# Moving half of VectorE's look-ahead statistics behind the normalising step in a fused group-norm and hexagonal convolution

## The reference

```python
g = v.reshape(B_, 32, C_ // 32, H_, W_)
gn = (g - mean(g)) / sqrt(var(g) + 1e-5)          # over each group of 2 x 256 values
xp = pad(gn, 1);  xp[:, :, DST_R, DST_C] = xp[:, :, SRC_R, SRC_C]     # 30 wrapped edge points
up    = conv(xp, w_up * _UP, b_up)                 # 5 taps each, stride 2, 64 -> 64 channels
left  = conv(xp, w_left * _LEFT, b_left)
right = conv(xp, w_right * _RIGHT, b_right)
out[:, :, 0::2, 0::2], out[:, :, 1::2, 0::2], out[:, :, 1::2, 1::2] = up, left, right
return x + out * OUT_MASK
```

## Time and profile before

| | |
|---|---|
| median of the runs | 735.11 us |
| profiled execution | 734.9 us |
| its span | 733.1 us |
| PE busy | 655.4 us (89%) |
| DVE busy | 617.0 us (84%) |
| ACT busy | 575.0 us (78%) |
| POOL busy | 473.3 us (65%) |
| moved between HBM and SBUF | 269.65 MB, mean 368 GB/s |
| granted TensorE clock, mean | 0.992 of full speed |

### The profile page before, as it was taken

How to read it: one execution, slowest core, us unless ns; L and a number is a source line. 1 busy time by engine, 2 the same in 40 slices (tenths; PEclk the granted TensorE clock), 3 DMA queues, 4 the chain that set the end, 5 groups by cost and what they waited for, 6 DMA issues and landing times.

```text
span 733.1 us, 36312 instructions
## 1 busy us (share of the span) xinstructions
PE 655.4 (89%) x15484; PEld 602.6 (82%) x15484; DVE 617.0 (84%) x1793; ACT 575.0 (78%) x1235; POOL 473.3 (65%) x1109
## 2 busy tenths in 40 slices
PE   1699999999999989889898898898988988988993
PEld 1589999999999888788788887887888878878883
DVE  4999999999999888798888888878988988878740
ACT  3498888988888787877877877878778778787782
POOL 1177777787777756757657557566576575675774
PEclk9999999999999999999999999999999999999997
DMA  8999999999999999999999999999999999999998
GB/s 265 348 360 384 384 384 379 373 375 372 370 370 373 371 375 372 365 373 374 371 381 381 368 376 377 371 361 376 378 375 377 375 375 376 372 362 374 383 353 285
DMA packets 271100, 269.65 MB, mean 368 GB/s; under 512 B 8720, under 2 KB 270864, under 8 KB 271056
## 3 DMA queue, kind: packets, MB, share of 16 engines
q1 hardware_dynamic: 270576, 269.25, 106.6%
q10 hardware_dynamic: 480, 0.00, 0.0%
HBM read 135.01 MB, written 134.22 MB: 367 GB/s over the span
## 4 chain that ended last, share of the span: by engine, by line
DVE 36%; DMA 25%; POOL 18%; ACT 12%; issue 3%; PE 3%; SPq 2%; POOLq 0%
DMA xs<-in_x 25%; DVE stats L246 19%; POOL xs L418 13%; ACT tn L330 12%; DVE tn L294 8%; POOL tn L428 5%; PE bank L476 3%; DVE small L278 2%; SPq L197 2%; DVE small L282 2%; DVE rstd L285 2%; DVE nmr L289 1%; DVE mate L254 1%; DVE var L267 0%; DVE small L275 0%
## 5 line engine op out<-in xcount | busy, mean ns | idle before, releaser
L476 PE MATMUL bank<-tn,wts 64*64 64x192 f32 (+1 forms) x15360 | 646.6, 325 | 0.0
L476 PEld LDWEIGHTS bank<-tn,wts 64*64 64x64 f32 x15360 | 593.2, 136 | 34.0
L246 DVE BATCH_NORM_STATS2 stats<-xs 128x6 f32<-128x512 f32 x512 | 350.6, 697 | 84.8 <-DMA xs<-in_x 84.4
L418 POOL TENSOR_TENSOR xs<-res,xs 128x192 f32<-128x192 f32 (+6 forms) x775 | 375.1, 528 | 5.7 <-ACT res L353 4.6
L330 ACT ACTIVATE tn<-xs,nmr,rstd 128x256 f32<-128x256 f32 x511 | 258.9, 592 | 74.1 <-DVE nmr L289 73.6
L353 ACT ACTIVATE res<-bank,bias 64x512 f32<-64x512 f32 (+5 forms) x640 | 302.1, 472 | 18.1 <-PE bank L476 7.7
L428 POOL COPY tn<-tn 128x128 f32<-128x128 f32 (+2 forms) x320 | 97.9, 362 | 238.2 <-ACT tn L330 238.2
L294 DVE TENSOR_SCALAR tn<-xs,rstd,nmr 128x256 f32<-128x256 f32 x513 | 180.3, 424 | 2.3
L487 PEld LDWEIGHTS bank<-blank 128*128 128x128 f16 x64 | 6.1, 96 | 76.3 <-ACT res L353 58.7
L487 PE MATMUL bank<-blank 128*128 128x2 f16 x64 | 11.2, 176 | 57.8 <-POOL tn L428 57.8
L324 ACT ACTIVATE std<-var 128x16 f32<-128x16 f32 x64 | 13.8, 216 | 50.7 <-DVE var L267 50.7
(11 more groups left out here) (18 smaller groups left out, 24.0 us busy)
## 6 DMA issues: line engine op xcount, KB each, us to landing
xs<-in_x SPq DMA_DIRECT2D x256, 512.0 KB, 8.0
out<-xs SPq DMA_DIRECT2D x256, 512.0 KB, 8.3
tn<-in_L_conv_w_up SPq DMA_DIRECT2D x1, 256.0 KB, 3.6
tn<-in_L_conv_w_left SPq DMA_DIRECT2D x1, 256.0 KB, 4.1
tn<-in_L_conv_w_right SPq DMA_DIRECT2D x1, 256.0 KB, 5.5
bias<-in_L_conv_b_up ACTq DMA_DIRECT2D x2, 0.2 KB, 4.5
bias<-in_L_conv_b_left ACTq DMA_DIRECT2D x2, 0.2 KB, 5.6
bias<-in_L_conv_b_right ACTq DMA_DIRECT2D x2, 0.2 KB, 7.3
```

What stands on the lines that cost most here:

```text
L246: last = nc.vector.bn_stats(stats[:, k % 2, 2 * u:2 * u + 2].rearrange("p g a -> p (g a)"), both)
L418: last = nc.gpsimd.tensor_tensor(onto, frm, onto, ALU.add)
L476: last = nc.tensor.matmul(psum[bank + j][to:to + C, at:at + cols], wts[first:first + C, NT * rect[0] + n, :], taps(b, rect, tap, first), s ...
```

## The change

In `moments` and `norms` DVE now takes only the first four of the next chunk's eight `bn_stats`, one in each of four places. The other four, with their wait for the second half of that chunk's load, follow `normalise(k)`.

```diff
-                bn(ahead, 2, 4)
+                bn(ahead, 2, 3)
 
             def norms(k, ahead):
                 dve.wait_ge(std_ready, k + 1)
                 nc.vector.reciprocal(small[:, 0], std[:]).then_inc(stat_step, 1)
-                bn(ahead, 4, 5)
+                bn(ahead, 3, 4)
                 dve.wait_ge(stat_step, done + 1)
                 nc.vector.scalar_tensor_tensor(small[:, 1], ...)
-                bn(ahead, 5, 6)
                 dve.wait_ge(stat_step, done + 2)
                 nc.vector.tensor_tensor(small[:, 2], ...)
-                bn(ahead, 6, 7)
                 dve.wait_ge(stat_step, done + 3)
                 nc.vector.scalar_tensor_tensor(rstd[:], ...)
-                bn(ahead, 7, 8)
                 dve.wait_ge(stat_step, done + 4)
                 nc.vector.scalar_tensor_tensor(nmr[:], ...)
...
                 moments(k, k + 1)
                 norms(k, k + 1)
                 normalise(k)
+                bn(k + 1, G // 4, G // 2)
                 if k + 1 < NCHUNK:
                     dve.wait_ge(bn_done, k + 2)
```

## The result

| | before | changed |
|---|---|---|
| median of the runs | 735.4 us (735.0 to 735.9, 4 runs) | 780.75 us (780.3 to 781.0, 4 runs) |
| span of the profiled execution | 733.1 us | 779.0 us |
| ratio, 95% interval | | 1.0611 (1.0596 to 1.0626) |
| DVE busy | 617.0 us | 729.9 us |
| var(2), var(63), start in us | 35.98, 698.32 | 36.33, 745.74 |

The change made the kernel 6.1% slower; forecast were 784 us, 6.6%. The spacings of chunks, here and in the experiments, are the differences of the starts of L267, of which there are 64 in each trace. Counted so, the chunk of the earlier trace rows is chunk 14, from var(14) to var(15), and not chunk 13.

The account below looks back on a forecast made before the run. DVE, held up by POOL's additions, was to bound every chunk: 36.5 to var(2), 61 steps of 11.7 (713.7) less 1.0, then 33.1, a span of 782.3 and a time of 784 us; range 752 to 798.

Parts of the forecast that it names:

- DVE becomes the bound for all chunks, through POOL's additions: DVE's two-input steps and `tn` wait for POOL's additions; DVE needs 11.7 us a chunk, against 11.2 for the transfers.
- The sum for a chunk: DVE from var to var: 7.4 to the last `tn`, 2.5 for four statistics, 1.7 from shuffle to var, 11.6 us.
- Before, DVE spends the additions on three of the small steps: Kernel before: during POOL's additions DVE does four statistics, three small steps and half of the `tn`.
- Four small steps go with four additions, eight `tn` with eight: L278, L282, L285 and L289 each wait for one POOL addition; the eight `tn` go with additions 5 to 12.
- The copies cost 0.1: POOL's wrap copies beside two-input steps L258 to L262: between 0 and 0.3 us a chunk, taken as 0.1.
- var(2) at 36.5, the last step 1.0 shorter, 33.1 from var(63) to the end: Start and end of the run, in us: var(2) about 0.5 later, last spacing 1.0 shorter, tail 33.1 instead of 34.8.
- ACT waits for var by 2 us or more, PE idle 1.6, DMA share down: Signs in the changed profile: ACT and PE figures in us a chunk, DMA share at 11.2 / 11.7 of before.
- DVE sets the pace while it is ahead of the transfers: Kernel before, early chunks: DVE, at 10.16 us a chunk, was taken as the bound; later the transfers, at 11.2.
- A change that leaves DVE under 11.2 costs nothing in the middle: Middle of the run: transfers take 11.2 us a chunk, DVE 10.16, so DVE was said to have 1.0 us spare.
- the first rival: Transfers stay the bound if DVE's chunk stays under 11.2 us; only the tail gets shorter: 733 us, chance 0.11.
- That rival's tail gain of 2.1 us: PE starts its last two convolutions about 2 us sooner; the last four stores close a 2.1 us DMA gap.
- A smooth range between 10.16 and 11.7: Weaker collision in DVE's chunk: 11.35 us gives 763 us, chance 0.15; below 11.2 it turns into the first rival.

Follow-up runs that it names:

- short additions: POOL's additions cut to one image pair of sixteen, all twelve still issued: 739.49 us in the changed kernel, 737.66 us in the kernel before.
- a quarter less traffic: Half of each store left out, so a chunk moves 3 MB instead of 4: 778.77 us in the changed kernel, 686.56 us in the kernel before.
- short copies: POOL's wrap copies cut to one image pair of sixteen: before 738.24 us, changed 773.30 us, changed with second four statistics ahead of the `tn` 735.84 us.
- Two behind: From the kernel before, only the last two of the eight statistics go behind the `tn`: 758.89 us, ratio 1.0307.
- the run with chunk 62 alone: The kernel before with the changed order for chunk 62 only: 735.81 us against 736.02, ratio 0.9996.
- statistics ahead of the `tn`: The changed kernel with the second four statistics put between nmr and the `tn` instead of behind the `tn`: 757.66 us, ratio 1.0294.

## Why the prediction was right, and where it was not

- *DVE becomes the bound for all chunks, through POOL's additions.* Right, and shown from two sides: with short additions the order costs 1.8 us, with a quarter less traffic it costs the same as with all of it.
- *The sum for a chunk.* In us after var, forecast and measured in the chunk above: reciprocal 0.69 and 0.69, L278 1.40 and 1.40, start of the additions 1.16 and 1.03, their length 6.17 and 6.18, last `tn` done 7.4 and 7.36, four statistics 2.5 and 2.48 from there to the shuffle, shuffle to var 1.7 and 1.78. The chunk takes 11.62 us where I had 11.7 with the copies.
- *Before, DVE spends the additions on three of the small steps.* In the earlier trace rows it is all four: the additions end at 164.64, and the last small step ends before the `tn` start at 163.17. The sum does not use it.
- *Four small steps go with four additions, eight `tn` with eight.* Right, one by one. Each small step takes 0.50 to 0.57 us, and the `tn` end 0.15 us after the additions. In the middle of the run one `tn` takes a median of 521 ns.
- *The copies cost 0.1.* Only L259 met one, 252 ns in place of 174. With short copies the chunk is 0.10 us shorter, 11.53.
- *var(2) at 36.5, the last step 1.0 shorter, 33.1 from var(63) to the end.* Measured 36.33, 0.8 shorter (10.84) and 33.24. The forecast was 3 us over, which is the 0.06 a chunk by which 11.7 is over the measured mean of 11.64 from var(2) to var(62).
- *ACT waits for var by 2 us or more, PE idle 1.6, DMA share down.* ACT waited 2.55 us a chunk, PE 1.5, and the rate fell from 374 to 362 GB/s.
- *"DVE sets the pace while it is ahead of the transfers".* Not shown, and for the kernel before it does not hold: from 60 to 80 us PE is busy for 20.00 of 20 us as well. With short additions DVE is busy for only 44.5 of 50 us from 60 to 110 us, PE still for all 50, and the chunks come 10.09 us apart. So PE alone holds the early chunks at 10.1 us. How much less DVE itself would need beside full additions no run here shows. The sum of the forecast did not use this number.
- *"A change that leaves DVE under 11.2 costs nothing in the middle", and the first rival with its turning point at 11.2.* This step failed. It left out that the kernel before gains on the loads in its early chunks, and that at the end only stores are left, which wait for compute; the point is near the mean of 10.86 us, which stood in the paragraph before. Two behind, at 11.28, lost 23 us. The forecast did not hang on it, being over both. By this error the rival "the transfers stay the bound" had a place that was too wide, from 10.86 to 11.2.
- *That rival's tail gain of 2.1 us.* It was not had: PE's own queue of convolutions in the tail was left out, as the run with chunk 62 alone shows.
- *A smooth range between 10.16 and 11.7.* Not so: the loop through the copies, which I had priced at 0 to 0.3 us, sets 11.28 us as soon as three of L258 to L262 meet a copy. Two quite different orders landed on it.

The Trainium skill (SBUF — State Buffer, Who interferes with whom) has it that a VectorE instruction with at most one SBUF input, outside the two-port modes, does not contend with GpSimd, and that one with two SBUF inputs does, against a GpSimd instruction that reads SBUF. The runs agree: 684 to 698 ns for the statistics and 231 to 237 for the reciprocal on the pages of all kernels, and 0.17 against 0.5 us for the small steps by the length of POOL's instructions alone. The `tn` have one tensor input and are held up all the same, which the Trainium skill allows for in a two-port mode. No run here shows in which mode they are: beside short additions they take 0.33 us each for 256 values and the statistics 0.62 us for 512, so the `tn` are no faster a value.

No version faster than the kernel before was found. Its DMA engines are busy but for some 2 us at the end, and moving DVE's statistics for chunk 62 alone did not get them.

## What to carry to other kernels

Instructions of VectorE are not interchangeable beside a busy GpSimd: here `bn_stats` and `reciprocal` ran at full speed, while `tensor_scalar` and the steps with two inputs were paced one by one by GpSimd's instructions. Fill the stretch in which GpSimd is busy with the first kind, and look in the durations, not in the waits, for what the others lose. And where loads run ahead of compute and only stores are left at the end, do not take the pace of the middle, where the transfers are the bound, for what compute may take. Here the limit was near the mean over the whole run, 10.86 us a chunk and not 11.23, and 11.28 us cost 3.1%.

## What was not expected of the hardware

- A chain of dependent small steps locks to the other engine's instructions one for one: four steps of 0.17 us took 2.2 us beside additions, 0.55 each.
- Short waits of that kind can close a loop over three engines with a fixed period: 11.28 us in two orders (statistics ahead of the `tn`, and two behind). In the first of them short copies opened the loop, and the chunk fell to 10.68 us.
- With less work on GpSimd the kernel before became slower, by 0.2% (additions short) and 0.4% (copies short), at a lower rate of the transfers in the middle (11.31 and 11.32 us a chunk, not 11.23). The cause is open.
